# Graph network kernel: the backward messages of the last layer are made in destination order and scattered as rows, in place of records scattered beforehand and a second gather

## The reference

```
ht    = einsum('ne,reh->rnh', x, weights[-1])       # 18 tables of 3125 x 128
msg_f = ht[type, src]     + bias[type]              # forward,  one row per edge
msg_b = ht[type + 9, dst] + bias[type + 9]          # backward, one row per edge
out   = segment_sum(msg_f, dst) + segment_sum(msg_b, src)
```

## Time and profile before

| what | us |
|---|---|
| median of three runs | 5430.65 (5418.2 to 5432.55) |
| span of the profiled execution | 4651.0 |
| median less span | 779.65 |
| GpSimd busy in the span | 3414.1 (73%) |
| TensorE busy | 2871.3 (62%) |
| VectorE busy | 2230.8 (48%) |

### The profile page before, as it was taken

The page is one execution under the profiler, slowest core; times in us unless marked ns, Lnnn a source line. Parts: engine busy times, 40 slices in busy tenths (PEclk is TensorE's granted clock), DMA queues, the critical chain, the costliest instruction groups (busy, mean ns, idle before and its releaser), DMA issues. The chain is left out here.

```text
span 4651.0 us, 50018 instructions
## 1 busy us (share of the span) xinstructions
PE 2871.3 (62%) x13750; PEld 2210.0 (48%) x13751; DVE 2230.8 (48%) x2711; ACT 613.9 (13%) x1076; POOL 3414.1 (73%) x3213
## 2 busy tenths in 40 slices
PE   3799998967777777751989643444444333333333
PEld 1688887943333333331989433333333333333333
DVE  7899997656666666668971621111111111111112
ACT  0355554010000000001751000000000000000000
POOL 1888886857777777767867677777777777777775
PEclk8899999968877878875999866666666566555556
DMA  6466566816666666651989523222222122212221
GB/s 191 139 189 183 170 187 209 265 37 172 170 170 170 170 171 173 173 153 59 278 241 276 174 68 94 68 68 68 68 68 68 49 53 52 53 53 53 53 53 51
DMA packets 498663, 599.91 MB, mean 129 GB/s; under 512 B 190115, under 2 KB 367441, under 8 KB 496248
## 3 DMA queue, kind: packets, MB, share of 16 engines
q0 software_dynamic: 117856, 246.12, 19.4%
q1 hardware_dynamic: 337751, 229.77, 17.7%
q10 hardware_dynamic: 42944, 122.68, 7.3%
HBM read 406.69 MB, written 204.36 MB: 131 GB/s over the span
## 5 line engine op out<-in xcount | busy, mean ns | idle before, releaser
L1151 PE MATMUL ps<-got,g_hot 128*128 x3224 | 719.2, 414 | 1151.3 <-DMA got<-y_back,s_msg 597.5
L721 POOL DMA_INDIRECT rec_by_src<-rec,pos x782 | 1123.9, 1437 | 344.1 <-issue 245.8
L1151 PEld LDWEIGHTS ps<-got,g_hot 128*128 128x128 f32 x3224 | 667.8, 316 | 1213.1 <-issue 1213.1
L1612 POOL DMA_INDIRECT sc_kv<-kv,d_src x806 | 762.0, 945 | 254.9 <-issue 245.3
L1036 POOL DMA_INDIRECT got<-y_forward,d_msg x782 | 739.1, 945 | 238.2 <-issue 238.2
L1036 POOL DMA_INDIRECT got<-y_back,s_msg x766 | 722.7, 943 | 241.7 <-issue 233.1
L806 PE MATMUL ps<-ln_low,ln_hot 128*125 128x256 f32 x2848 | 618.9, 380 | 19.7 <-DVE ln_low L783 15.9
L806 PEld LDWEIGHTS ps<-ln_low,ln_hot 128*125 128x125 f32 x2848 | 535.3, 188 | 103.2 <-issue 22.7
L1059 DVE TENSOR_TENSOR g_hot<-ps,src_loc 128x1024 f32<-128x1024 f32 x101 | 123.4, 1224 | 832.1 <-PE ps L1151 831.7
L1715 PE MATMUL ps<-q,sc_hotT 128*128 x1616 | 274.2, 322 | 236.4 <-DVE sc_hotT L1657 207.4
L1067 DVE TENSOR_TENSOR g_y<-ps,ms_b 128x384 f32<-128x384 f32 x75 | 41.8, 558 | 732.1 <-PE ps L1164 732.1
(11 more groups left out here) (328 smaller groups left out, 3102.4 us busy)
## 6 DMA issues: line engine op xcount, KB each, us to landing
linked<-ln_out SPq DMA_DIRECT2D x320, 224.0 KB
ve<-sc_kve ACTq DMA_DIRECT2D x202, 256.0 KB
wv_ve<-ve SPq DMA_DIRECT2D x101, 512.0 KB, 5.0
l_links<-linked SPq DMA_DIRECT2D x25, 800.0 KB, 7.3
l_links<-linked ACTq DMA_DIRECT2D x25, 800.0 KB, 9.2
attr_pairs<-ln_feats POOLq DMA_DIRECT2D x7, 2048.0 KB
sc_attr<-attr_pairs SPq DMA_DIRECT2D x202, 64.0 KB, 2.6
sc_kv<-kv,d_src POOLq DMA_INDIRECT x806, 3.0
```

The lines of the kernel that those rows point to most:

```text
L721: pool.indirect_dma_start(out=dram["rec_by_src"], out_offset=bass.IndirectOffsetOnAxis(ap=S["pos"][:, c:c + 1], axis=0), in_=S["rec"][:, c ...
L1151: last = pe.matmul(ps[:, bass.ds(columns[j], width)], hot[:, q, j, :], got[:, bass.ds(slots[j], width)], start=False, stop=True, skip_grou ...
L1612: pool.indirect_dma_start(out=kv[:, q, j, :], out_offset=None, in_=dram["kv"], in_offset=bass.IndirectOffsetOnAxis(ap=S["d_src"][:, c:c + ...
```

## The change

The record scatters, `sort_by_block` and the second gather go. The backward messages are made where dst order makes their table rows contiguous: a window of 14 nodes by 9 relations is 126 rows of `y_back`, read with one plain DMA, and a one-hot of (dst, type) picks the rows of a tile's edges by matmul. ScalarE copies each chunk of four tiles out of PSUM with the local src number as column 128, and GpSimd scatters the rows (132 floats, 528 bytes) to the src order in `back_rows`. That order now starts each src block at a full tile, so that at most 806 tiles are read back, in sequence, by plain DMAs. One `gather_sum` then sums forward gathers and these rows side by side. `norm_and_messages` makes the backward table now, and the forward one is made beside the scatters.

`back_plan` replaces `sort_by_block` and holds its chain (masks, counts, scan, 25 `copy_predicated`) after the same steps for windows of 14 nodes (eight counts over 782 columns, step tables, keys); it reads the tiles' first nodes, so `file_records`, which writes the records and reads these, is a stage of its own before it.

```diff
+def file_records(nc, S, dram):          # a stage: write rec_by_dst, wait, read firsts, wait
+    ...
+def clear_rows(nc, sp, S, dram, blanked):            # SyncE, beside the first mlp_layer
+    spare = BACK_TILES + 1 - TILES                   # 25 tiles in one DMA
+    sp.dma_start(dram["back_rows"]...[:, TILES:, :], S["blank_row"]...).then_inc(blanked, 16)
+    sp.wait_ge(blanked, 16)
+    for k in range(BLOCKS):
+        tail = sp.value_load(S["back_tails"][0:1, k:k + 1], min_val=0, max_val=BACK_TILES * P)
+        sp.dma_start(dram["back_rows"][bass.ds(tail, P), :], S["blank_row"][:, :]).then_inc(blanked, 16)
+        sp.wait_ge(blanked, 16 * (k + 2))
+def back_plan(nc, S, dram):
+    ...
+            link(dve.tensor_tensor(climb[:, :], climb[:, :], ps[:, 0:TILES], ALU.add))
+            for c in range(M_BLOCKS):                # 8
+                link(dve.tensor_scalar(below[:, :], climb[:, :], limit[:, c:c + 1], 0.0, ALU.is_lt, ALU.add, accum_out=count[:, c:c + 1]))
+    ...
+            for k in range(BLOCKS):
+                dve.wait_ge(ranked, k + 1)
+                dve.copy_predicated(place[:, :], mask[:, k, :].bitcast(U16), rank(k)).then_inc(chose, 1)
-def send_some(pool, S, dram, first, last):
-    ...
+def send_back(nc, S, dram):                          # M_STEPS 253 steps of 4 pairs, 196 chunks of 4 tiles
+        # SyncE, step n:
+            def load_keys(n):
+                if n >= M_WAYS:                      # 8
+                    sp.wait_ge(spread, n - M_WAYS + 1)
+                sp.dma_start(key_rows[0:1, n % M_WAYS, :], dram["back_keys"]...).then_inc(placed[n % M_WAYS], 16)
+            def load_table(n):
+                if n >= M_WAYS:
+                    sp.wait_ge(paired, n + 1)
+                _, at = nc.values_load_multi_w_load_instructions(...)
+                for j in range(M_STEP):              # 4 DMAs of 126 rows
+                    sp.dma_start(table[0:M_KEYS, n % M_WAYS, j, :], source[bass.ds(at[j], M_KEYS), :]).then_inc(landed[n % M_WAYS], 16)
+        # GpSimd:
+            for c in range(M_CHUNKS):
+                pool.wait_ge(stocked, c + 1)
+                pool.nop(nofuse=True)
+                for j in range(size(c)):
+                    t = c * M_CHUNK + j
+                    pool.indirect_dma_start(out=dram["back_rows"], out_offset=bass.IndirectOffsetOnAxis(ap=S["pos"][:, t:t + 1], axis=0),
+                                            in_=rows[:, c % RING_ROWS, j, :], in_offset=None).then_inc(sent[c % RING_ROWS], 16)
+        # VectorE: clears ps, rows (8 chunks) and zero first; then step n:
+                dve.wait_ge(spread, n + 1)
+                dve.wait_ge(paired, n + 1)
+                dve.tensor_scalar(hot_t[0:M_KEYS, n % M_WAYS, :], spread_of(n)[0:M_KEYS, :], S["part"][0:M_KEYS, 0:1], None, ALU.is_equal).then_inc(heated, 1)
+        # ScalarE, chunk c: waits until its last step is summed and the rows of chunk c - 8 are sent
+                act.activation(rows[:, q, 0:size(c), D:D + 1], S["back_loc"]..., ACT.Copy).then_inc(evicted, 1)
+                act.activation(rows[:, q, 0:size(c), 0:D], chunk(c)..., ACT.Copy).then_inc(evicted, 1)
+                act.wait_ge(evicted, 2 * (c + 1))
+                act.activation(chunk(c), zero[:, :], ACT.Copy).then_inc(cleared, 1)
+                act.sem_inc(stocked, 1)
+        # TensorE, step n: 4 matmuls, then the spread of the keys of step n + 2;
+        # every tenth step three pieces of 384 columns of the forward table
+    ...
 def gather_sum(...):
+        # SyncE: one plain DMA per group of 8 tiles of back_rows, four groups ahead
+                sp.wait_ge(taken[q], i + 1)
+                sp.dma_start(back[:, q, 0:back_in(n), :], back_tiles[:, n * GROUP:n * GROUP + back_in(n), :]).then_inc(brought[q], 16)
+        # GpSimd: the 782 forward gathers, as g3 had them
+        # VectorE: compare(i, k) and compare_back(i, k) for each group
             with pe.Fori(0, WHOLE) as i:
                 for k in range(RING):
+                    back_group(i, k)
                     landed_group(i, k, GROUP)
-        @block.gpsimd                                # in nine stages
-        def _(pool):
-            send_records(pool, S, dram, tag)
+        if first:                                    # mlp_layer
+            @block.sync
+            def _(sp):
+                clear_rows(nc, sp, S, dram, m.sem(tag + "_blank_rows"))
-                gather_sum(nc, S, dram, "g3", "dst", tables[0], S["d_msg"], (tables[1], S["s_msg"]))
-            gather_sum(nc, S, dram, "g4", "src", tables[1], S["s_msg"])
+                send_back(nc, S, dram)
+            gather_sum(nc, S, dram, table)
```

More of the change, by code:

```diff
@@ L598, in _ @@
             act.wait_ge(kept, len(outputs))
[L601 to L606, removed]
+def file_records(nc, S, dram):
     with ExitStack() as stack:
         m = Memory(nc, stack)
[L609 to L623, removed]
-        order, ready, marked, added, asked, told, split, spread, ranked, chose = (m.sem("sb_" + n) for n in (
-            "order", "ready", "marked", "added", "asked", "told", "split", "spread", "ranked", "chose"))
-        moved, fetched = m.sem("sb_moved"), m.sem("sb_fetched")
-        rv = S["rec"][:, :].rearrange("p (c r) -> p c r", r=REC)
-        ps = S["ps"]
@@ L926, in load_columns @@
     return values
-def gather_sum(nc, S, dram, tag, name, table, index, second=None):
-    width, WAYS = D, 4
-    GROUPS = -(-PAIRS // GROUP)
-    TILE_GROUPS = -(-TILES // GROUP)
-    WHOLE, REST = divmod(GROUPS, RING)
-    back = second is not None
-    shift = 0 if back else TILE_GROUPS % RING
-    earlier = [0 if back else 16 * sum(min(GROUP, TILES - g * GROUP) for g in range(r, TILE_GROUPS, RING)) for r in range(RING)]
-    got, landed = S["got"], S["landed"]
+def send_back(nc, S, dram):
+    RING_ROWS = 8
+    PER = 10
@@ L1051, in _ @@
+            for q in range(RING_ROWS):
+                pool.wait_ge(sent[q], 16 * sum(size(c) for c in range(q, M_CHUNKS, RING_ROWS)))
         @block.vector
         def _(dve):
[L1053 to L1060 removed]
+            dve.memset(ps[:, 0:M_REGIONS * BANK], 0.0).then_inc(blank, 1)
@@ L1138, in _, with back_group @@
                 pe.sem_inc(summed[q], 1)
-            if back:
-                pe.wait_ge(cleared, 1)
+                pe.sem_inc(taken[q], 1)
+            pe.wait_ge(cleared, 1)
+            def back_group(i, k, tiles=GROUP):
+                q, turn = k % WAYS, i * (RING // WAYS) + (k // WAYS + 1)
+                _, columns = nc.values_load_multi_w_load_instructions(
+                    S["back_cols"][0:1, bass.ds(start_of(i, k), tiles)], engines=[mybir.EngineType.PE], min_val=0, max_val=(BLOCKS - 1) * D,
+                    skip_runtime_bounds_check_because="block numbers are counts of blocks")
+                pe.wait_ge(warmed[q], turn)
+                pe.wait_ge(brought[q], turn * 16)
+                for j in range(tiles):
+                    last = pe.matmul(ps[:, bass.ds(columns[j], D)], back_hot[:, q, j, :], back[:, q, j, 0:D],
+                                     start=False, stop=True, skip_group_check=True)
+                last.then_inc(taken[q], 1)
```

738 lines of the change are left out of this document (415 added, 323 removed).

## The result

The changed kernel takes **5578.1 us** (median of four runs, 5570.8 to 5588.1) against 5428.1 for the kernel before in the same job: a ratio of 1.0279, 95% interval 1.0261 to 1.0298, 150 us more. The forecast was 5553, 122 us more. The direction is right and the size is near; the way there is not, because the profile on which the prediction rests is of an execution that no timed run repeats. The kernel before, profiled once more, has a span of 5407.4 us for a run of 5409.2; in the first profile it was 4651.0. One other execution of the kernel before, among those timed for the comparison with the moved scatters, took 9497.7 us; the ratio there leaves it out.

The account below looks back on a forecast made before the run. GpSimd's gathers were taken as the limit in g3 and g4 (1955 of 1982.8 us). Plan 70, clearing 26 and `send_back` with `gather_sum` 26 add 122 to 5430.65: 5553 us, range 5490 to 5690.

Parts of the forecast that it names:

- record scatters out: Stages with record scatters: removing them gives 0 us, since PE or VectorE hides them.
- plan for sort: `file_records` and `back_plan` replace `sort_by_block`: that stretch ends at 149 in place of 78.6, +70 us.
- `clear_rows`: First `mlp_layer`: 25 clearing DMAs in series on SP take 80 us against 53.3 idle, +26 us.
- `send_back` for g3: Stage replacing gather sum g3: GpSimd's 782 row scatters at 1.275 us set it, 1012 us in all.
- `gather_sum` for g4: Stage replacing gather sum g4: 782 gathers at 1.250 us plus start and end, 997 us; back tiles hidden on PE.
- the rest: Other stages, such as `norm_and_messages`, which makes the other table half at the same size: 0 us.
- 779.65 above the span: Whole kernel: the runs' median exceeds the profile's span by 779.65 us, carried over unchanged to the changed kernel.
- The bound from below: Removed record scatters: if they caused all idle time of six stages' busiest other engines, 108 us would go.
- Relief: Rival, 0.08: record scatters hold up their stages; removing them gives back up to 108 us, +14 net, 5445 us.
- The landing: Clearing on SP: each of 25 DMAs waits 2.4 us to land; the skill's fit estimates 2.16 us.
- The step chain bounds `send_back`: Rival, 0.10: semaphore hops through SP, PE, VectorE, PE, ScalarE cost 5.07 us a step, 1283 us, +286: 5839.
- VectorE holds up the row scatters: Rival, 0.06: in `send_back`, VectorE's some 232 busy us make GpSimd stand still, about +130 us: 5683.

Follow-up runs that it names:

- the moved scatters: Kernel before with all 782 record scatters, moved out of the first mlp_layer, project, mlp_and_linked_sum's MLP part and norm_and_messages: 5471.1 us, ratio 1.010.
- the chain alone: Changed kernel with send_back's 782 row scatters left out and back_rows filled with zeros in the first mlp_layer: send_back takes 840 us.
- the scatters alone: Changed kernel's send_back with only the 782 row scatters, of zeros, and the forward table; keys, step tables, one-hots, step matmuls, evictions left out: stage 1089 us.

## Why the prediction was right, and where it was wrong

The forecast's terms beside what the runs show (us):

| term | forecast | measured | from |
|---|---|---|---|
| record scatters out | 0 | -228 (timed: -220) | second profile of before, without record scatters |
| plan for sort | +70 | +70 | until `index_stage`, 148.9 against 79.3 |
| `clear_rows` | +26 | +15 | m0 68.9 against 54.2 |
| `send_back` for g3 | +21 | +256 | 1377.1 against 1121.5 |
| `gather_sum` for g4 | +6 | +48 | 1176.9 against 1128.9 |
| the rest | 0 | +6 | |
| sum | +122 | +166 of spans, +150 of medians | |

So the sum is near by luck: two large errors of opposite sign, 228 us in one direction and 277 in the other, nearly cancel. Point by point:

**"The runs' median is 779.65 above the span; no view shows what lies there, so I carry it over."** This step failed first, and the errors at the record scatters and the gathers follow from it. Nothing lies there: the timed runs spend that time inside the stages, in GpSimd's above all. A span 14% below the run's time said that the profile and the times were not of the same behaviour. The number that this gave, 5430.65 as the base, was right all the same.

**"Record scatters out: 0 us."** Wrong by 220. In the first profile they are hidden; in the timed runs the stages around them are slowed. The bound from below, 108 us, came from idle time in rows of the same profile and could not hold. The rival *Relief*, with 8%, had the sign and half of the size.

**The plan, +70.** Right to the microsecond: the cast of the places ends at 148.4, the stage at 148.9, forecast 149.

**`clear_rows`, +26.** The mechanism is right (SP still clears when VectorE is through at 1071.3; `project` starts at 1087.3), the size is not: the 25 turns are (1083.5 - 1026.7) / 24 = 2.37 us each in place of 2.83, and the whole takes 68 in place of 80. The landing was the disputed term. The Trainium skill's fit for GpSimd's path ("DMA: Bandwidth & Descriptors", "Anatomy of one DMA"), by which the prediction estimated the clearing at 74, was the nearer of the two, and still too long.

**`send_back`, 1012.** The price of a row scatter is right (0.968 + 0.30 = 1.27), and the claim that the others keep under 3.94 us a step holds for the chain alone: 3.3. The step that failed is the one from there to the stage, that the slower of the two sets it and neither touches the other. Its term for SyncE, "about 2.6" a step (its parts add up to 2.3), was taken from `scores` in the first profile; alone the fastest steps take 2.9, and beside the scatters SyncE needs 1377 / 253 = 5.4, almost without a wait. The steps run late, ScalarE with them, and GpSimd then waits 359 us for ScalarE, which is what the prediction named as the sign against it. The rival *The step chain bounds `send_back`* (10%, 5.07 us a step, 1283 us) was right that the chain sets the stage; its reason, the hops between engines, was not, since the chain alone takes 840. The rival *VectorE holds up the row scatters* is out: they are 0.968 us busy. By the Trainium skill ("SBUF — State Buffer", "Who interferes with whom") they should not be held up by this one-hot, and the trace agrees.

**`gather_sum`, 997.** "So they are free, and would cost only if PE's 7.3 grew past 10." PE's work did not grow: it is busy 590.65 / 101 = 5.8 us a group, but a group takes 1176.9 / 101 = 11.7, and most of the rest is PE's idle time that ends with "issue". The back half is some 52 us, of which the register loads that the term left out are some 20; the other 134 (1125 against 991) are the base's error.

**The rest** stayed as forecast: `link_nodes` and the sums are as long as in the kernel before without record scatters, within 5 us, `scores` too.

What is not shown is why the scatters and gathers slow PE and SyncE, and why the first profile of before has none of it: GpSimd's gathers are as dense there, and none of its register instructions took 0.66 to 0.74 us. In the later traces SyncE and PE have such, VectorE and ScalarE none. Scatters beside `weigh_values` do not slow PE in either profile; there the record scatters are 1.50 us busy, the DMA engines at 0.90 and PE at full clock. The clock is 0.50 in the slow stretches, but it is so in the chain alone too (0.51), which has none. No experiment separated issue, descriptors and semaphores. Every timed run here has a span and a clock from the profiler, so whether the same pace holds without it is not shown either.

## What to carry to other kernels

Before the first sum is made, compare the profile's span with the run times: a span that is 14% shorter than every run is not overhead outside, it is another execution, and it has to be profiled again. When two engines are each fast enough alone, don't take the slower one as the stage's time before both have run together; here 840 and 1089 made 1377. Ask too which engine never waits, also when its work isn't counted as busy: here it was SyncE. And dense indirect DMAs from GpSimd can have a price for PE and SyncE beside them that GpSimd's own busy time doesn't show, so taking them out can be worth more than hiding them.

## What the runs showed of the hardware

- Beside GpSimd's back-to-back indirect DMAs PE can fall to one weight load or matmul per 0.70 or 1.40 us, 22 times fewer than after them, with no wait in the profile and DMA at 0.06. In the one stage looked at closely it set in some 12 us after the first of them and ended 10 us after the last one's packets.
- SyncE is slowed in the same step: 299 of its 2024 register instructions in `send_back` took 0.66 to 0.74 us in the changed kernel, none without the scatters, where they take 0.03. VectorE and ScalarE had none.
- Half of the scatters, with waits between, cost the chain 86 us; all of them 490 to 540. With a memset of 0.22 us between them the stage was shorter than in any of four without.
- The recorded end of a matmul is no proof of its result: VectorE started 3.3 us behind it.
- A row scatter is shorter beside other work than alone. In the kernel with the scatters alone it takes 269.32 / 274 = 0.98 us while the forward table is made, and 555.46 / 509 = 1.09 once nothing else runs (GpSimd's busy us, count, clock, DMA share, GB/s). With the 0.30 between them that is one per 1.40 us, PE's slow step; whether the two have one cause is not shown.

```profile
2998.00:3362.00 364.00, 269.32 (x274) 0.50 0.25 90
3362.00:4087.00 725.00, 555.46 (x509) 0.50 0.14 48
```

- PE that is busy 760 of 840 us, in the chain alone, was granted 0.51 of the clock on average (the lower level, 1.2 GHz), while the sum in `mlp_and_linked_sum` gets 0.95.
